# A decoder layer on one core: in the cross attention, the maxima 2.9 groups ahead of the scores and the transposition of the shift 0.3 of a group behind them

## The reference

```
xn1 = ln(x, g1, be1);  sa = mha(xn1, xn1, Wq_s.., causal=True);    x = x + sa @ W1 + b1
xn2 = ln(x, g2, be2);  ca = mha(xn2, ctx, Wq_c.., causal=False);   x = x + ca @ W2 + b2
xn3 = ln(x, g3, be3);  x = x + relu(xn3 @ Wf1 + bf1) @ Wf2 + bf2

mha: q, k, v = projections;  scores = q k^T / (D ** -0.5)          # that is, times 4
     attn = softmax(scores);  out = attn v                          # per head
```

## Time and profile before

| | us |
|---|---|
| median of three runs | 598.66 (596.15 to 600.23) |
| the profiled execution | 595.19 |
| its span | 593.3 |
| PE busy | 492.2 (83%) |
| DVE busy | 334.3 (56%) |
| ACT busy | 322.1 (54%) |
| POOL busy | 189.5 (32%) |

### The profile page before, as it was taken

One profiled execution on the slowest core, in us unless ns is written; L12 is line 12 of the kernel. 1 busy time (PEld: TensorE's weight loads), 2 busy tenths in 40 slices (PEclk: granted clock), 3 DMA queues, 4 the chain that ended last, 5 costly groups with the idle time before them and its releaser, 6 DMA issues.

```text
span 593.3 us, 8855 instructions
## 1 busy us (share of the span) xinstructions
PE 492.2 (83%) x3296; PEld 281.7 (47%) x3296; DVE 334.3 (56%) x645; ACT 322.1 (54%) x622; POOL 189.5 (32%) x291
## 2 busy tenths in 40 slices
PE   1588974999999999999998867867786577999887
PEld 1485641343434343434343235432323366988877
DVE  3165985877778777787841225654541466263340
ACT  3685311767676767676766750245673753344360
POOL 2497970121212121213131352423323273030200
PEclk9998997999999999999998998778887978999999
DMA  8145945025261616160205037376733310101001
GB/s 278 60 130 180 222 129 104 1 40 89 43 112 43 98 34 115 31 114 9 68 19 161 0 95 175 91 160 114 115 76 76 75 39 0 36 2 36 19 19 35
DMA packets 31082, 48.11 MB, mean 81 GB/s; under 512 B 8832, under 2 KB 25728, under 8 KB 28928
## 3 DMA queue, kind: packets, MB, share of 16 engines
q1 hardware_dynamic: 30904, 47.52, 34.9%
q10 hardware_dynamic: 136, 0.03, 0.1%
HBM read 30.66 MB, written 12.03 MB: 72 GB/s over the span
## 4 chain that ended last, share of the span: by engine, by line
PE 58%; DMA 15%; DVE 9%; ACT 8%; issue 3%; POOL 2%; SPq 2%; ACTq 0%; DVEq 0%
PE ps L974 12%; PE ps L1096 12%; PE ps L1066 10%; PE ps L1029 9%; PE ps L1183 8%; DMA stacks<-shift_t 5%; DMA sums<-out_t 4%; DVE max_a L1262 4%; DMA recips<-recip_rows 4%; PE ps L958 3%; ACT arena_p L832 3%; PE ps L1051 2%; PE ps L1033 2%; ACT out_t L843 2%; DMA recip_rows<-sums 1%
## 5 line engine op out<-in xcount | busy, mean ns | idle before, releaser
L832 ACT ACTIVATE arena_p<-ps 128x512 f32<-128x512 f32 (+4 forms) x416 | 194.6, 537 | 121.8 <-PE ps L1066 120.4
L1262 DVE TENSOR_REDUCE max_a<-ps 128x1 f32<-128x512 f32 (+4 forms) x280 | 161.9, 621 | 65.0 <-PE ps L1029 49.5
L1066 PE MATMUL ps<-stacks 99*128 99x512 bf16 (+1 forms) x448 | 140.5, 347 | 32.8 <-DMA stacks<-shift_t 24.9
L1029 PE MATMUL ps<-stacks 96*128 96x77 bf16 (+4 forms) x640 | 137.5, 287 | 11.7 <-DVE max_a L1262 8.2
L1096 PE MATMUL ps<-arena_p,v_group 128*32 128x512 f32 (+3 forms) x896 | 99.8, 524 | 1.6 <-POOL arena_p L699 1.2
L699 POOL TENSOR_SCALAR_AFFINE_SELECT arena_p<-arena_p 128x512 f32<-128x512 f32 x64 | 39.9, 635 | 177.4 <-ACT arena_p L832 177.4
L1029 PEld LDWEIGHTS ps<-stacks 96*128 96x128 bf16 x640 | 53.8, 103 | 87.9 <-DVE max_a L1262 48.5
L1066 PEld LDWEIGHTS ps<-stacks 99*128 99x128 bf16 x448 | 42.5, 100 | 92.0 <-ACT arena_p L832 46.2
L1262 DVE TENSOR_REDUCE max_b<-ps 128x1 f32<-128x384 f32 (+3 forms) x88 | 52.4, 634 | 6.7 <-PE ps L1033 6.6
L1242 DVE TENSOR_TENSOR xs<-ps,xs 128x512 f32<-128x512 f32 x24 | 16.4, 690 | 68.8 <-PE ps L974 45.7
L908 ACT ACTIVATE hid_r<-ps,col 128x512 fp32r<-128x512 f32 x32 | 22.0, 688 | 54.0 <-PE ps L1183 51.7
(11 more groups left out here) (73 smaller groups left out, 520.6 us busy)
## 6 DMA issues: line engine op xcount, KB each, us to landing
arena_h<-out_t SPq DMA_DIRECT2D x16, 256.0 KB, 5.3
recips<-recip_rows SPq DMA_DIRECT2D x8, 512.0 KB
q_parts<-parts SPq DMA_DIRECT2D x8, 384.0 KB, 2.7
k_parts<-parts SPq DMA_DIRECT2D x8, 384.0 KB, 2.9
qc_parts<-parts SPq DMA_DIRECT2D x8, 384.0 KB, 3.6
stacks<-qc_parts SPq DMA_DIRECT2D x8, 384.0 KB, 6.0
stacks<-q_parts SPq DMA_DIRECT2D x7, 384.0 KB, 4.9
stacks<-k_parts SPq DMA_DIRECT2D x7, 384.0 KB, 7.6
```

Of the source, the lines that this page charges most:

```text
L832: nc.scalar.activation(probs[0:a.kp, a.probs_slot(g, ui), h, k * BANK:k * BANK + width], ps[0:a.kp, unit % S_BANKS, 0:width], ACT.Exp, sca ...
L1029: ins = nc.tensor.matmul(m_bank(use)[:, o:o + w], q_stack[0:ROWS, g % a.nb, h, t * P:(t + 1) * P], k_rows(ROWS, g, h, s0, s0 + w), start=T ...
L1066: ins = nc.tensor.matmul(ps[:, unit % S_BANKS, lo - k * BANK:hi - k * BANK], k_rows(ROWS_S, g, h, i * P, (i + 1) * P) if a.causal else k_c ...
L1262: nc.vector.tensor_reduce(dst, m_bank(use)[:, 0:nh * w].rearrange("p (h w) -> p h w", h=nh), AX.X, ALU.max).then_inc(s.max_read, 1)
```

## The change

Two constants of the cross attention's order: the lead of the maxima over the scores goes from 2.3 to 2.9 groups, and the distance of the shift's transposition behind its maxima from 0.5 to 0.3 of a group. The self attention is not touched, and the keys of the row products move with the lead, so that their places among the scores stay.

```diff
-CROSS = Attention(False, S_CTX, buffers=5, lead=2.3, gap=0.5, rows=[(7.05, 7.15, 7.55), (7.6, 7.7, 7.99)])
+CROSS = Attention(False, S_CTX, buffers=5, lead=2.9, gap=0.3, rows=[(7.05, 7.15, 7.55), (7.6, 7.7, 7.99)])
```

## The result

The changed kernel takes 602.24 us, median of 14 runs (598.86 to 604.63), against 599.45 us for the kernel before in the same session (594.35 to 600.86): a ratio of 1.0055, 95% interval 1.0028 to 1.0081. It is slower, by 0.3 to 0.8%, and not by the 1.5% that was forecast. Timed again on two other chips with six runs each, it is 1.0103 (1.0055 to 1.0150) and 1.0098 (1.0063 to 1.0132) of the kernel before. The three intervals overlap, so they show no difference between the chips. The profiled execution took 604.63 us.

A forecast was written before the change was run, and what follows sets the result against it. PE was taken as the engine to follow, with 18.6 us of shift waits and the reciprocals' chain ending together at the first row product. Delays there summed to +9.0 us, plus the distance to the median: 607.5 us, range 599 to 613.

The forecast's parts named there:

- A, the start: Start of cross attention: group 0's shift transposition overtakes the last normalised quarter's and waits for POOL; whole 2.1 us taken.
- B, one buffer: DVE's copy into the single shift buffer waits for shift 1's landing, stopping PE; group 1's scores at 411.0 against 405.00.
- C, loads behind the shift: On SP a stack's last load queues behind the shift; PE waits 3.7 us at group 5's first maxima, then 3.0.
- D, the reciprocals: Store of first reciprocals comes late on SP; first division ends 446.5 against 437.47, first row product at 462.5.
- Sum: First row product at 462.5 less 453.46, +9.0 us, plus the profiled execution's 3.5 us distance to the median: 607.5 us.
- the figure of 2.3 us: Skill page's landing time for a 128 KB load; would give back 3.0 us, 604.5 in all; nothing hangs on it.
- What follows R0.0: Everything after the first row product: same order and waits as before, so nothing added.
- Rival 1: Stack loads land in time and cost nothing: first row product at 453.8, +0.3, 599.0 us, not slower; chance 0.17.
- rival 2: Shift was the bound, both spreads land in 1.5 us, first row product not held: 588.9 us; chance 0.05.
- Rival 3: All PE waits followed by half clock, and congestion at the reciprocals' store: upper bound, 611.6 us; chance 0.15.

The follow-up runs named there:

- after_loads012: Changed kernel with the three loads of a stack at score units 0, 1 and 2 in place of 0, 2 and 4: 1.0059 of the kernel before.
- after_again: Changed kernel, no edit, profiled a second time: 85.6 us from the first maxima to the first row product.
- after_all3: Changed kernel with the early list cut at 11, a second shift buffer and stack loads at units 0, 1, 2: 1.0004 of the kernel before.

## Why the prediction was right or wrong

**A, the start: place right, size not shown.** The transposition began 7.9 us into the stage in place of 5.7, so 2.2 us later, with 2.1 forecast. What it is worth in time is 1.5 us by the ratio and 0.4 by the median, and not clear of zero.

**B, one buffer: right.** PE stopped at c3.5 as worked out, s1.0 came 33.8 us into the stage (408.55 less 374.80) where 34.2 was forecast, and SH3 (411.39) 36.6 where it was 36.8. Taken away it gives 2.9 to 4.4 us, by the medians the most of the three. The wait ahead of SH1, 2.56 us, was overlooked; the places of s1.0 and SH3 came out right all the same, since both wait for the landing of shift 1.

**C, loads behind the shift: right in place and sum.** c5.0, c6.0 and c7.0 waited 3.49, 1.98 and 3.17 us (3.7 and 3.0 forecast for the first two), with half clock after the first and full clock after the second, as taken. c5.0 came 43.3 us into the stage, forecast 43.5. Its terms were less good than their sum, which is in part luck. The landing of the last load, taken as 3.9 us, was 3.2, 3.0 and 3.1, and SP's three issues, taken as 1.8, took from 1.9 to 2.9 (the first of them 411.93, the load behind them 414.78). The 3.9 is the median of loads in the order of before; with an earlier issue the same loads take 7 (after_loads012).

**D, the reciprocals: right in form.** The first division ended 70.7 us into the stage (69.7 forecast), R0.0 came at 86.8 (85.7), and the 16.0 us between came out as 16.1. The 1.0 us more comes mostly with the first store, which landed after 2.7 us and not after 1.5. Over five profiles the mean of R0.0 is 85.4.

**Sum: this is the step that failed.** "462.5 less 453.46 is +9.0 us" set the new stage against one execution of before, and that execution had the short course: 76.7 us, where the mean of five is 79.0 and three of five take 80.1 to 81.3. Against the mean the same working gives +6.7, and +6.4 was measured on the profiles. The end of the step counted the same 2.3 us a second time: "I add the difference to that" carried the 3.5 us between the profiled execution and the median of before over to the changed kernel. The profiled execution of before was low in part because its stage was short, which the changed kernel's never is. Counted once, the forecast is 605.4 us; without the addition it is 604.2, and the changed kernel's five profiled executions took 604.6, 605.0, 601.3, 603.9 and 602.3. (The sum also has a slip: 604.2 and 3.5 are 607.7, not 607.5. And what the figure of 2.3 us would give back, with 3.9 in the sum, is twice 1.6, so 3.2 and not 3.0.) What follows R0.0, put at nothing, took 0.5 us more in the mean of five profiles. The short base accounts for 2.3 us of the miss. The rest, +6.7 against the +2.8 to +4.7 of the medians or the 3.3 to 6.2 of the ratios, is open, as said above.

**Rivals.** Rival 1 (the loads land in time, 599.0) and rival 2 (588.9) are out: the waits for stacks<-qc_parts stand in all five profiles, and no spread took less than 7.4 us in them. Rival 3, everything at half clock, did not happen. The estimate of 2.3 us for a 128 KB load is from the fit in the Trainium skill ("DMA: Bandwidth & Descriptors", Anatomy of one DMA), which the page gives for GpSimd's queue. For the loads from SP here no time as short was seen: in the profile of the changed kernel all loads of stacks took 3.0 to 7.1 us, and the 128 KB ones that PE waited for 3.0 to 3.2, which is nearer to that estimate than to the 3.9 of the sum.

## What to carry to other kernels

A forecast that sums waits from one profiled execution inherits the course which that execution took; where waits decide whether PE goes on at half clock, profile the kernel more than once, and do not add the distance to the median on top. When work is put further ahead, list for each stage what it now overtakes on every in-order queue and which single buffers sit between: here the start, one buffer of shifts and the place of the loads made up the whole cost, and removing six waits gained nothing visible, as R0.0 then waits for the division. And where a chain holds an instruction, move it behind work that is ready: the two kernels with that step stand 0.5 to 0.6% below the one without, and the lead alone gave nothing.

## What the runs showed of the hardware

The same program took two courses through one stage, 76.2 to 76.7 and 80.1 to 81.3 us, with the granted clock at 1.00 in one and 0.56 in the other over the same 7 us, after idle times of 1.88 and 6.37 us. And the loads of a stack (128 to 384 KB, one queue) landed between 2.9 us (after_again) and 9.5 us (after_all3) after their issue.
